# Graph attention on one core: each gather of a chunk's rows waits for its own step count

## The reference, cut to what matters

```python
e = jax.nn.leaky_relu(a_s[:, src] + a_d[:, dst], NEG_SLOPE)
m = jax.ops.segment_max(e_h, dst, num_segments=N)
ex = jnp.exp(e_h - m[dst])
den = jax.ops.segment_sum(ex, dst, num_segments=N)
alpha = ex / den[dst]
out = jax.ops.segment_sum(h_h[src] * alpha[:, None], dst, num_segments=N)
```

## Time and profile before

| | us |
|---|---|
| median of 3 runs (1752.55 to 1759.93) | 1753.17 |
| the profiled execution's own time | 1735.01 |
| its span | 1733.3 |
| first product's addition to the last (turns 2 to 38) | 256 to 976 |
| PE / DVE / ACT / POOL busy over the span | 1223.4 / 1054.4 / 478.1 / 664.4 |

### The profile page before, as it was taken

One profiled execution on the slowest core, in us unless ns is written; L12 is line 12 of the kernel. 1 busy time (PEld: TensorE's weight loads), 2 busy tenths in 40 slices (PEclk: granted clock), 3 DMA queues, 4 the chain that ended last, 5 costly groups with the idle time before them and its releaser, 6 DMA issues. The chain is left out here.

```text
span 1733.3 us, 29694 instructions
## 1 busy us (share of the span) xinstructions
PE 1223.4 (71%) x6248; PEld 985.7 (57%) x6249; DVE 1054.4 (61%) x2961; ACT 478.1 (28%) x1894; POOL 664.4 (38%) x756
## 2 busy tenths in 40 slices
PE   0697056776778778877787506999998099999700
PEld 0475034554556556555565306989987089999700
DVE  7667224564667666676777565799986334444267
ACT  1342021222222222332222015555552022323210
POOL 2100546555556453554540003465565111111164
PEclk9998557787899887997878757999998599999955
DMA  6014635665667565775664444334441493222155
GB/s 215 20 35 69 140 90 163 185 187 165 190 198 213 177 212 160 210 226 181 204 201 149 116 144 167 122 116 142 143 138 63 160 370 118 70 70 70 54 153 153
DMA packets 220207, 258.18 MB, mean 149 GB/s; under 512 B 57157, under 2 KB 193864, under 8 KB 216392
## 3 DMA queue, kind: packets, MB, share of 16 engines
q1 hardware_dynamic: 174328, 137.65, 25.2%
q0 software_dynamic: 30848, 103.40, 20.5%
q10 hardware_dynamic: 14928, 16.00, 2.8%
HBM read 142.03 MB, written 114.93 MB: 148 GB/s over the span
## 5 line engine op out<-in xcount | busy, mean ns | idle before, releaser
L702 POOL DMA_INDIRECT rows<-node_rows,srcT x391 | 383.4, 980 | 329.1 <-PE pO L1003 207.8
L1003 PE MATMUL pO<-rows,pw 128*128 x1184 | 366.1, 442 | 62.7 <-DVE pw L792 29.4
L808 DVE SCALAR_TENSOR_TENSOR acc<-acc,rsc,pO 128x257 f32<-128x257 f32 x592 | 281.5, 476 | 169.3 <-PE pO L1003 56.1
L1003 PEld LDWEIGHTS pO<-rows,pw 128*128 128x128 f32 x1184 | 235.5, 219 | 112.6 <-issue 81.6
L1344 PE MATMUL pW_<-W_again,aT 128*128 128x256 f32 x800 | 182.2, 381 | 0.0
L1344 PEld LDWEIGHTS pW_<-W_again,aT 128*128 128x128 f32 x800 | 149.2, 191 | 18.5
L1679 PEld LDWEIGHTS pHe<-xeT,w1e 128*128 128x128 f32 x1056 | 129.7, 194 | 8.6 <-DVE w1e L1717 4.3
L1679 PE MATMUL pHe<-xeT,w1e 128*128 128x128 f32 x1056 | 130.4, 277 | 4.5 <-DVE xeT L1697 4.5
L1735 POOL DMA_DIRECT2D ys_rows<-ye x66 | 35.9, 544 | 240.2 <-DVE ye L1727 240.2
L1688 PE MATMUL pYe<-w,hT 128*128 x528 | 125.4, 380 | 0.4 <-issue 0.4
L1658 ACT ACTIVATE hT<-pHe,b 128x128 f32<-128x128 f32 x264 | 75.5, 368 | 180.4 <-PE pHe L1679 153.7
(11 more groups left out here) (323 smaller groups left out, 1972.9 us busy)
## 6 DMA issues: line engine op xcount, KB each, us to landing
agg_rows<-acc SPq DMA_DIRECT2D x296, 256.0 KB
w<-in_ffn_w SPq DMA_DIRECT2D x32, 512.0 KB, 5.5
xe<-xs_rows ACTq DMA_DIRECT2D x66, 128.0 KB, 2.1
ys_rows<-ye POOLq DMA_DIRECT2D x66, 128.0 KB, 2.0
rows<-node_rows,srcT POOLq DMA_INDIRECT x391
node_rows<-xna SPq DMA_DIRECT2D x25, 136.0 KB
xna<-in_x SPq DMA_DIRECT2D x5, 640.0 KB, 12.1
mix_rows<-hx SPq DMA_DIRECT2D x25, 128.0 KB
```

Source lines behind the costliest of these rows:

```text
L702: pool.indirect_dma_start(rows[:, k % RING, :], None, node_rows[:, :], at_row(srcT[:, k:k + 1])).then_inc(s_rows[k % len(s_rows)], 16)
L808: dve.scalar_tensor_tensor(out=acc[:, k % V3, s % HG, 0:D + 1], in0=before, scalar=rsc[:, g % V2, s:s + 1], in1=pO[n % PB][:, 0:D + 1], op ...
L1003: pe.matmul(pO[n % PB][:, 0:D + 1], pw[:, s // HG, s % HG, :], rows[:, ds(at[s % 4], 1), 0:D + 1].rearrange("p c f -> p (c f)"), start=Tru ...
```

## The change

Three things, all about when POOL may issue gather k. (`FLY` = 4 is the number in flight, as before.)

1. `free_at` holds a number for each chunk, and every gather from k = 4 on loads its own and waits for `prod` before it is issued.
2. `prod` no longer starts at 0 with the first product. PE raises it by 1 at the start of the stage, and in turns 0 and 1 it raises it by a portion's size at each place where later turns have that portion of products. So it stands at 1 + 2 * 16 = 33 when the products begin. All who wait for `prod` through `Count` have 33 added.
3. The number is the larger of two: chunk k-40's last step must be done (from k = 40 on), and the last step of chunk k-4 must lie fewer than `LEAD` = 48 steps ahead. In steps done (that is `prod` less 33): at least `ends[1][k-40] + 1` and at least `ends[1][k-4] - 47`.

```diff
-RING, FETCH = 40, 4
-FETCHES = -(-CHUNKS // FETCH)
+RING, FLY, LEAD, AHEAD = 40, 4, 48, 2
...
-                    line.do(dve.memset(free_at[:, :], 1))
-                    line.do(dve.tensor_scalar(free_at[:, RING // FETCH:FETCHES], ends[:, 1, FETCH - 1:FETCH * (FETCHES - RING // FETCH):FETCH], 1.0, None, ALU.add))
+                    line.do(dve.tensor_scalar(may_go[:, FLY:CHUNKS], ends[:, 1, 0:CHUNKS - FLY], float(2 + AHEAD * G - LEAD), 1.0, ALU.add, ALU.max))
+                    line.do(dve.scalar_tensor_tensor(out=may_go[:, RING:CHUNKS], in0=ends[:, 1, 0:CHUNKS - RING], scalar=2.0 + AHEAD * G, in1=may_go[:, RING:CHUNKS], op0=ALU.add, op1=ALU.max))
+                    line.do(dve.tensor_copy(free_at[:, FLY:CHUNKS], may_go[:, FLY:CHUNKS]))
...
-            pw_in, prod, acced, den_in = Count(sem("pw_in"), 2), Count(sem("prod"), G), Count(sem("acced"), G), Count(sem("den_in"))
+            pw_in, prod, acced, den_in = Count(sem("pw_in"), 2), Count(sem("prod"), G, 1 + AHEAD * G), Count(sem("acced"), G), Count(sem("den_in"))
...
-                        if k >= RING and k % FETCH == 0:
-                            steps = pool.value_load(free_at[0:1, k // FETCH:k // FETCH + 1], min_val=1, max_val=GROUPS * G)
+                        if k >= FLY:
+                            steps = pool.value_load(free_at[0:1, k:k + 1], min_val=1, max_val=(GROUPS + AHEAD) * G + 1)
                             pool.wait_ge(prod.sem, steps)
...
+                    pe.sem_inc(prod.sem, 1)
                     pe.wait_ge(v_cw, 1)
...
-                    groups([(1, out_proj), product(0, 2), (1, scores), product(2, 5), (1, last_heads), (0, num), product(5, 7), (1, carries), product(7, 9), (1, turn_back), (0, eq_turn),
-                            product(9, 12), (1, shares), product(12, 14), (1, tops), (0, turn), product(14, 16)])
+                    def fill(lo, hi):
+
+                        return 0, lambda g: pe.sem_inc(prod.sem, hi - lo) if g < AHEAD else None
+
+                    groups([(1, out_proj), fill(0, 2), product(0, 2), (1, scores), fill(2, 5), product(2, 5), (1, last_heads), (0, num), fill(5, 7), product(5, 7), (1, carries), fill(7, 9), product(7, 9), (1, turn_back), (0, eq_turn),
+                            fill(9, 12), product(9, 12), (1, shares), fill(12, 14), product(12, 14), (1, tops), (0, turn), fill(14, 16), product(14, 16)])
```

More of the change, by code:

```diff
@@ L225, in build @@
         step_tab = sb("step_tab", [1, SP_ // G, TAB], I32, edge_ctx)
-        free_at = sb("free_at", [1, FETCHES], I32, edge_ctx)
+        free_at = sb("free_at", [1, CHUNKS], I32, edge_ctx)
         step_chunk = dram("step_chunk", (2, SP_), I32)
@@ L237, in build @@
             junk = sb("junk", [P, C1], ctx=ctx)
+            may_go = sb("may_go", [1, CHUNKS], ctx=ctx)
             cs = sb("cs", [P, 6, SJ], ctx=ctx)
@@ L651, in build @@
             consts.expect(7)
-            s_rows = [sem(f"s_rows{c}") for c in range(4)]
+            s_rows = [sem(f"s_rows{c}") for c in range(FLY)]
             s_flg, s_top = [sem(f"s_flg{c}") for c in range(V2)], sem("s_top")
```

## The result

The changed kernel takes 1690.28 us (median of 4 runs, 1687.48 to 1693.59); the kernel before took 1756.55 in the same session (4 runs, 1752.55 to 1764.96). The ratio is 0.968, with a 95% interval of 0.9639 to 0.972. The forecast was 1704.

The account below looks back on a forecast made before the run. Neither PE nor DVE was full; edge-stage turns were taken as lengthened by PE increments held during POOL's unbroken gather runs. Shorter runs -50, DVE's numbers +1, so 1753.2 - 49 = 1704 us; range 1640 to 1768.

Parts of the forecast that it names:

- the first stretch: The edge stage's first six whole turns, 24.8 us each at 14 gathers; 17 of 51 us excess was to go.
- The first forty gathers: Start of the edge stage: DVE's 15.3 us wait in turn 1 would stay; gain 0, bound 14 us.
- The runs: POOL's unbroken rows of gathers in the edge stage: single releases shorten holds of PE's increments, gaining 50 us.
- Register loads, numbers, increments: POOL's 299 more loads cost 0, DVE's numbers +1 us, PE's 15 increments 0; bounds 25, 1.4 and 3.6 us.
- What would show it: Signs in the profile after: shorter turns, more but shorter POOL waits, no late-increment wait over 5 us behind turn 1.
- The floor: Edge stage's turn by itself, read from its last stretch without gathers: 16.25 us, leaving 125 us of excess.
- The mechanism: Edge stage: a PE increment can be held while POOL issues gathers without pause, until about the run's end; excess 125 us.
- No change: Rival for the edge stage: holds come from gathers in flight, not runs of them; 1754 us, chance 0.16.

Follow-up runs that it names:

- e3: The kernel before with the changed rules for gathers 4 to 39 only, batches of four by the old rule from 40 on; 1723.78 us, ratio 0.9955.
- e2: The changed kernel with all its rules, but one load and wait for each four gathers, for the fourth's number; 1713.9 us, ratio 0.9922.
- e1: The kernel before, but from chunk 40 on each gather waits for its own old chunk; no lead, no count from the first turn; 1702.64 us, ratio 0.9843.
- e8: The changed kernel without the lead rule from chunk 40 on, each gather there waiting for its own old chunk alone; 1692.53 us, ratio 0.9815.
- a_again: The repeat: the changed kernel run once more, unaltered, in a later session against the kernel before; 1684.17 us, ratio 0.9779.
- e10: The changed kernel with a one-element POOL memset ahead of each gather, in the last session; 1618.98 us, ratio 1.0168.
- e4: The changed kernel issuing no gathers from chunk 40 on, later products reading old rows; 1572.04 us, ratio 0.9095 to the kernel before.
- e6: The changed kernel with two gathers in flight instead of four; 1923.7 us, ratio 1.1156 to the kernel before.
- e9: The changed kernel with three gathers in flight instead of four; 1694.65 us, ratio 0.9685 to the kernel before.
- e11: The kernel before with three gathers in flight instead of four, batches of four and old rules kept; 1699.59 us, ratio 0.9724.
- e12: The changed kernel with three gathers in flight and the lead rule for the first 40 only, in the last session; 1680.79 us, ratio 1.0557.

## Why the prediction was right in its number, and where its steps were wrong

**The number.** Forecast 1704, range 1640 to 1768, faster with 0.65; measured 1690, faster by 3.2%. The forecast sum of -49 us stands against -46 in the profiled executions, -66 in the medians of the first session and -44 in those of the repeat. That the sum came so near in the profiled executions is luck: 13 us of turn 1 came unasked, 17 us of the first stretch stayed away, 4 and 6 us more came in the later ones, and some 9 were lost behind the stage.

**The first forty gathers: wrong.** "The 15.3 us of turn 1 stay: 0, with 14 us as the bound of a gain." It went, and 13 us came of it. (The 15.3 us are DVE's idle time; the matmul had ended 14.1 us before DVE's start.) The step was to say that a row still unbroken would still hold the increment. In the changed kernel the row was unbroken again at 229.7 and held nothing, and e3, which has this rule alone, has its first addition at 247.1. The one pause of 2.7 us some 4 us earlier may have been enough; that isn't shown, as e2 is held through pauses of 0.8 and 1.0 us.

**The runs: right in sum, wrong by place.** A third of the first stretch's excess (17 us) was to go; nothing went in the profiled execution, 9 us in the repeat (23.3 us a turn). Half of the second and third (30 us): 34 went. The fourth: 3 us forecast, 9 measured. The gain lies mostly where POOL has slack; where 14 gathers a turn leave it none, it is 0 to 9 us.

**What the gain is made of.** e1, own release, is worth 1.6%; e3, the first forty, 0.45%; the lead, by e8 against a_again, 0.4%. Together 2.4%, against 2.2% for the whole in the repeat. Batches kept (e2) leave 0.8% of it. So by the times the separate release is the main part, as the prediction had it. It is not shown beyond doubt: the intervals of e1 and e2 overlap, and e2's traced execution has turns as short as the changed kernel's without it.

**Register loads, numbers, increments: 0, right.** POOL's interval is still 1.25 us at its shortest with a load ahead of every gather. e10 hides nearly all of a memset there too.

**What would show it.** Turns of 18.5 in the second and third: 19.3 and 17.0. 21.9 in the first: missed, 24.9. POOL's waits for products: 116 for 60 and at most 3.8 us, as said. ACT on landed rows at most 22: 23.1, just over the bound. Late increments "none over 5 us behind turn 1": missed, ACT's L907 still waited up to 9.8, and of 171 us 127 are left.

**The floor: too high.** I took the last stretch's 16.25 us; e4 gives 14.9 where the other engines have the same work and nothing is gathered, at a granted clock of 1.00 instead of the last stretch's 0.87. From the first addition to the last the kernel before took 720 us and e4 560, so the excess was some 160 us and not 125.

**The mechanism: right that gathers delay PE's increments, wrong that an unbroken row is what does it.** For it: next to no late increments without gathers (e4), fewer with more pauses (e1, a_again), none with two in flight (e6). The pauses came as forecast: counting gathers under 1.45 us apart as one row, from gather 40 on, a row has 4.0 gathers on average before and 2.0 in the changed kernel (at most 12 and 8). Against it: the unbroken row of the changed kernel at 229.7; e10's, as far as a session that may hold nothing counts; and e2, whose rows have 3.9 gathers and whose held time is the changed kernel's. The trace of the kernel before itself had the plainest case against it. Its row in turn 1 runs from gather 14 at 211.4 us to gather 39 at 242.99, and in this same row an increment of PE came through at once, 1.7 us before the held one:

```profile
226.69 0.95 POOL L702 DMA_INDIRECT rows<-node_rows,srcT  x1 [0.31 <-issue]
...
229.03 0.22 PE L963 MATMUL pC<-lastm,cst 128*8 128x16 f32 x2 [3.22 <-ACT lastm L884]
...
229.29 0.23 DVE L752 TENSOR_TENSOR_SCAN co<-stepT,co,pC 8x16 f32<-8x16 f32 x1 [1.64 <-issue]
```

What decides when an increment is held stays open. e9 and e11 both have three in flight; with each gather released by itself 11.6 us are late, with batches 107.3. They differ in the rule for the first forty and in the lead too, so that both thinning out and the number in flight matter is likely, not shown. "No change", the rival that put it all on gathers in flight, was wrong in its result, but its premise holds a part: fewer in flight, fewer holds. The rule of the Trainium skill that I set beside it (SBUF — State Buffer, "SBUF: two separate sides": TensorE doesn't wait for the port pair or for DMA) isn't contradicted, since PE's matmul in turn 1 ran on time; but it says nothing on the way of the increment, and the gathers as a whole cost 9% here (e4).

**Two rivals that nobody named.** One is that the holds depend on where and when the kernel runs. In the last session they seem not to exist, and the nearest relative of the changed kernel, e10, was 1.7% slower than before. Why is open: ACT waited 97.3 us for landed rows there (34 times, at most 7.3), which points at the later releases, but the memset wasn't tried alone. The other is that recording the events makes the holds or moves them, since they go with missing records. No run was set up to part the two.

## What to carry to other kernels

When an engine waits for an increment whose instruction has long ended, look at what POOL issues beside it, and try the number of indirect DMAs in flight first: one constant did nearly as much in e11 as the rules of the change. It has its price: with two in flight the kernel was 11.6% slower, and e12, with three, 5.6% slower in the last session. A floor is better measured, by leaving the transfers out, than read from the stage's quiet end. And a gain that comes from such waits should be timed in more than one session before it is kept, since a session that seems to have been without them gave the kernel before 8 to 9% and turned two relatives of the faster kernel into slower ones.

## What the runs showed of the hardware that I had not expected

- Increments of PE reached DVE and ACT up to 14.1 us after the end of their matmul (kernel before; 14.8 in e2) while POOL issued indirect DMAs with four in flight, about as often with rows of 32 bytes as of 1088 (50 and 45 waits), and never over 1 us late with two in flight.
- In the same traces most of the gathers' landing updates are not recorded (2161 of 6256), and in traces without late increments most or nearly all are (5060 to 6240). That both have one cause, a crowded path of semaphore updates, is my guess, not shown.
- An indirect DMA of 128 rows takes POOL 1.25 us in an unbroken row, with or without a register load ahead of it, and 1.28 on average with a one-element memset as well (e10).
- The kernel before took 1728 to 1757 us in four sessions and 1590 in the fifth.
- The two kernels with separate releases and three in flight are close, 1694.7 us in a session with late increments elsewhere (e9, with lead) and 1680.8 in the one without (e12, no lead); they differ in the lead rule, so this is no clean comparison.
